# Weights of all experts loaded into the attention's raw weight buffers, and the experts' loops written out

## The reference

```python
x = x + attention(layernorm(x), ctx)      # 64 x 128 tokens of 512; 16 heads of 128, 4 key/value heads,
                                          # q and k RMS-normed, softmax over 128 context rows
x = x + experts(layernorm(x))
def experts(h):                           # T = 8192 tokens, E = 12 experts, top 2, F = 64
    rw, sel = top_k(softmax(h @ gate_w.T), 2); rw = rw / rw.sum(-1)
    for e in range(E):                    # at most cap = ceil(T / E * 1.25) = 854 tokens each
        tok, w = the first cap (token, slot) pairs that chose e
        out[tok] += w * (silu(h[tok] @ w1[e].T * (h[tok] @ w3[e].T)) @ w2[e].T)
```

## Time and profile before

| | |
|---|---|
| three timed runs | 2479.02, 2481.12 (median), 2481.80 us |
| the profiled execution | 2481.03 us, span of its instructions 2479.3 us |
| busy over the span | PE 92%, DVE 76%, ACT 71%, POOL 43% |
| mean granted TensorE clock | 0.963 of 2.4 GHz |
| attention (part one) | from 0 to 2162.2 us |
| experts (part two) | from 2162.3 us to the end |
| DMA | 348 MB, 140 GB/s in the mean |

### The profile page before, as it was taken

How to read it: one execution, slowest core, us unless ns; L and a number is a source line. 1 busy time by engine, 2 the same in 40 slices (tenths; PEclk the granted TensorE clock), 3 DMA queues, 4 the chain that set the end, 5 groups by cost and what they waited for, 6 DMA issues and landing times. The chain is left out here.

```text
span 2479.3 us, 54980 instructions
## 1 busy us (share of the span) xinstructions
PE 2279.2 (92%) x12931; PEld 1143.6 (46%) x12931; DVE 1877.1 (76%) x5158; ACT 1749.1 (71%) x6911; POOL 1055.1 (43%) x1949
## 2 busy tenths in 40 slices
PE   3899999999999999999999999999999999468875
PEld 1344444444444444444444444444444444234442
DVE  6787888888888888888888888888888887436554
ACT  5777777777777777777777777777777777334432
POOL 4333333343343333333443433333333433368875
PEclk9999999999999999999999999999999999878876
DMA  8476666666666666666666666666666666459997
GB/s 254 90 145 138 137 139 135 135 135 136 139 137 136 144 140 138 141 134 136 134 137 137 139 136 140 144 137 138 136 137 135 135 136 126 95 144 188 184 176 92
DMA packets 894359, 348.03 MB, mean 140 GB/s; under 512 B 829004, under 2 KB 829260, under 8 KB 894288
## 3 DMA queue, kind: packets, MB, share of 16 engines
q1 hardware_dynamic: 867520, 297.06, 56.4%
q0 software_dynamic: 22912, 43.16, 9.8%
q10 hardware_dynamic: 3888, 7.38, 0.8%
HBM read 91.37 MB, written 57.71 MB: 60 GB/s over the span
## 5 line engine op out<-in xcount | busy, mean ns | idle before, releaser
L813 PE MATMUL pb<-wo,o 128*128 128x512 f16 x3072 | 708.3, 380 | 21.7 <-DVE o L1065 14.9
L744 PE MATMUL pb<-wq,xT 128*128 128x512 f16 x3072 | 709.0, 381 | 2.1 <-DMA xT<-x 1.2
L943 ACT ACTIVATE work<-pb,small 128x128 f32<-128x128 f32 x1024 | 455.2, 453 | 353.7 <-DVE small L1128 353.7
L1396 POOL TENSOR_TENSOR small<-small 128x4 f32<-128x4 f32 (+1 forms) x584 | 484.1, 833 | 60.9 <-POOL small L1467 18.4
L744 PEld LDWEIGHTS pb<-wq,xT 128*128 128x128 f16 x3072 | 300.8, 98 | 367.3 <-DVE q L1116 13.6
L813 PEld LDWEIGHTS pb<-wo,o 128*128 128x128 f16 x3072 | 286.0, 98 | 357.6 <-DVE o L1065 30.8
L1467 POOL TENSOR_TENSOR small<-small 128x4 f32<-128x4 f32 x256 | 52.1, 203 | 902.0 <-ACT junk_q L924 896.5
L744 PE MATMUL pb<-wkv,cT 128*128 128x512 f16 x1536 | 377.1, 382 | 2.9 <-DVE wkv L1282 2.9
L1116 DVE SCALAR_TENSOR_TENSOR q<-pb,small,q 128x128 f16<-128x128 f32 x1024 | 288.3, 344 | 76.2 <-ACT q L933 76.2
L933 ACT ACTIVATE q<-pb,small 128x128 f16<-128x128 f32 x1024 | 291.1, 366 | 6.3 <-DMA qT<-q 6.3
L1060 DVE TENSOR_TENSOR p<-work,p 128x512 f16<-128x512 f32 x256 | 177.3, 692 | 142.9 <-ACT p L951 137.1
(11 more groups left out here) (146 smaller groups left out, 2887.9 us busy)
## 6 DMA issues: line engine op xcount, KB each, us to landing
work<-x SPq DMA_DIRECT2D x128, 256.0 KB, 2.8
work<-c SPq DMA_DIRECT2D x64, 256.0 KB
out<-work SPq DMA_DIRECT2D x64, 256.0 KB, 2.0
xn_scratch<-work SPq DMA_DIRECT2D x64, 256.0 KB, 2.1
wo_raw<-wo ACTq DMA_DIRECT2D x4, 1024.0 KB, 9.3
qT<-q SPq DMA_TRANSPOSE x256
pT<-p SPq DMA_TRANSPOSE x256
wq_raw<-wq ACTq DMA_DIRECT2D x3, 1024.0 KB, 11.6
```

The lines of the kernel that those rows point to most:

```text
L744: mm = nc.tensor.matmul(bank[:, :], lhs[:, NC * a + c, :], rhs[b_][:, c, :], start=(c == 0 and n == 0), stop=(c == NC - 1 and n == 2))
L813: mm = nc.tensor.matmul(WO_B[:, :], o16[:, HPG * a + h, :], part(O0 + g, b_)[:, h, :], start=(g == 0 and h == 0 and n == 0), stop=(g == NG ...
L943: ex = nc.scalar.activation(probs[:, cols], S_B[:, cols], ACT.Exp, bias=nmax[:, h:h + 1], scale=esc, accum_out=psums[:, h:h + 1])
L1396: return nc.gpsimd.tensor_tensor(out_, in_, neghalf[:, 0:n], ALU.pow)
```

## The change

All twelve experts' weights are loaded once, in part one, into the place of the raw query weights (w13: `w13_all`, 128 x 12 x 4 x 128) and of the raw output weights (w2: `w2_all`, 128 x 12 x 512), which stay allocated through part two. SP issues the three DMAs of an expert at the end of slots 0 and 2 of bodies 2, 61, 62, 63, 64 and 65; ahead of the first it waits for all weights to be split. One semaphore counts them; PE, ACT and DVE wait for all 36 DMAs at the head of part two (PE after the matmul of the totals). The loads, buffers and waits of the weights leave part two, and with them SP's waits for `h_done` and `w2_lo_done`. The loops over pairs of experts of all five engines are written out with constants.

```diff
@@ experts, block.sync
-            def load_w13(j, i):
-                sp.dma_start(w13_s[i][:, :, :], w13[2 * j + i]).then_inc(d_w13[i], 16)
-
-            def load_w2(j, i):
-                for half in (slice(0, F), slice(F, 2 * F)):
-                    sp.dma_start(w2_s[i][half, :], w2T[2 * j + i]).then_inc(d_w2[i], 16)
...
                 wait_apart(sp, (xg_used[1 - i], j + i + 1))
                 load_from(*n)
-                wait_apart(sp, (h_done, 2 * (2 * j + i + 2)))
-                load_w13(*n)
-
-            def ahead_2(j, i):
-
-                wait_apart(sp, (w2_lo_done, 2 * j + i + 1))
-                load_w2(j + 1, i)
...
-            for i in range(2):
-                load_w13(0, i)
-                load_w2(0, i)
             sp.wait_ge(s_n, 1)
...
-            sp.wait_ge(h_done, 2)
-            load_w13(1, 0)
             for i in range(2):
                 ahead_3(0, i)
-                ahead_2(0, i)
                 if i == 1:
                     ahead_1(0, i)
-            with sp.Fori(1, PAIRS - 2) as j:
+            for j in range(1, PAIRS - 2):
                 for i in range(2):
                     ahead_3(j, i)
-                    ahead_2(j, i)
                     ahead_1(j, i)
@@ experts, block.gpsimd
-            with pool.Fori(1, PAIRS - 2) as j:
+            for j in range(1, PAIRS - 2):
@@ experts, block.tensor
-                pe.wait_ge(d_w13[i], 16 * (j + 1))
...
+            pe.wait_ge(d_wexp, 48 * E)
             transposes(0, 0)
             up(0, 0)
             step(0, 0)
             step(0, 1)
-            with pe.Fori(1, PAIRS - 1) as j:
+            for j in range(1, PAIRS - 1):
@@ experts, block.scalar (block.vector likewise)
-                act.wait_ge(d_w2[i], 32 * (j + 1))
...
+            act.wait_ge(d_wexp, 48 * E)
...
-            with act.Fori(1, PAIRS - 1) as j:
+            for j in range(1, PAIRS - 1):
@@ build
+        w13_all = wq_raw[:, :, :, :].rearrange("p g c n -> p (g c n)")[:, 0:E * NC * 2 * F].rearrange(
+            "p (e c n) -> p e c n", e=E, c=NC)
+        w2_all = wo_raw[:, :, :, :].rearrange("p g c n -> p (g c n)")[:, 0:E * HID].rearrange("p (e n) -> p e n", e=E)
...
+                def expert_weights(e):
+
+                    if e == 0:
+                        sp.wait_ge(w_lo, NC * len(SPLIT))
+                    sp.dma_start(w13_all[:, e], w13[e]).then_inc(d_wexp, 16)
+                    for half in range(2):
+                        sp.dma_start(w2_all[half * F:(half + 1) * F, e, :], w2T[e]).then_inc(d_wexp, 16)
+
+                EXPERT_LOADS = {(b, g): ((2 * n + g // 2),) for n, b in enumerate((2, NB - 3, NB - 2, NB - 1, NB, NB + 1))
+                                for g in (0, 2)}
...
                         if g == 3 and live(b - 1):
                             store_xn2(b - 1)
+                        for e in at_slot(EXPERT_LOADS, b, g):
+                            expert_weights(e)
```

More of the change, by code:

```diff
@@ L31, with experts @@
 TINY = 1e-30
-def experts(nc, gt, w13, w2T, out):
+def experts(nc, gt, w13_all, w2_all, out):
     f32, f32r, i32 = mybir.dt.float32, mybir.dt.float32r, mybir.dt.int32
     ACT = mybir.ActivationFunctionType
-    wait, wait_apart, sem, pb, ident, ones_b, macc, xn2_d, table_d = (gt[k] for k in (
-        "wait", "wait_apart", "sem", "pb", "ident", "ones_b", "macc", "xn2_d", "table_d"))
+    wait, wait_apart, sem, pb, ident, ones_b, macc, xn2_d, table_d, d_wexp = (gt[k] for k in (
+        "wait", "wait_apart", "sem", "pb", "ident", "ones_b", "macc", "xn2_d", "table_d", "d_wexp"))
     with ExitStack() as ctx:
@@ L45, in experts @@
         tot, first_n = sb("tot", [128, E]), sb("first_n", [128, E], i32)
-        w13_s = [sb(f"w13_{i}", [128, NC, 2 * F]) for i in range(2)]
-        w2_s = [sb(f"w2_{i}", [2 * F, HID]) for i in range(2)]
         w2_hi, w2_lo, h_parts = sb("w2_hi", [2 * F, HID], f32r), sb("w2_lo", [F, HID], f32r), sb("h_parts", [2 * F, CP], f32r)
@@ L60, in experts @@
         d_join0 = [sem("d_joined_0"), sem("d_joined_1")]
-        d_w13 = [sem(f"d_w13_{i}") for i in range(2)]
-        d_w2 = [sem(f"d_w2_{i}") for i in range(2)]
         d_from = [sem(f"d_from{i}") for i in range(2)]
@@ L163, in _ @@
             for i in range(2):
-                ahead_2(PAIRS - 2, i)
                 ahead_1(PAIRS - 2, i)
@@ L234, in up @@
                     for c in range(NC):
-                        mm = nc.tensor.matmul(H_B[k][:, 0:hi - lo], w13_s[i][:, c, :], xgT[:, c, lo:hi],
+                        mm = nc.tensor.matmul(H_B[k][:, 0:hi - lo], w13_all[:, e, c, :], xgT[:, c, lo:hi],
                                               start=(c == 0), stop=(c == NC - 1))
@@ L312, in split_w2 @@
             def split_w2(j, i):
-                act.wait_ge(d_w2[i], 32 * (j + 1))
                 wait(act, down_done, 2 * j + i)
-                nc.scalar.copy(w2_hi[:, :], w2_s[i][:, :]).then_inc(w2_hi_done, 1)
+                nc.scalar.copy(w2_hi[:, :], w2_all[:, 2 * j + i, :]).then_inc(w2_hi_done, 1)
             def exp_g(j, i):
@@ L371, in silu @@
                         dve.wait_ge(w2_hi_done, e + 1)
-                        nc.vector.tensor_tensor(w2_lo[:, :], w2_s[i][0:F, :], w2_hi[0:F, :].bitcast(f32),
+                        nc.vector.tensor_tensor(w2_lo[:, :], w2_all[0:F, e, :], w2_hi[0:F, :].bitcast(f32),
                                                 ALU.subtract).then_inc(w2_lo_done, 1)
@@ L384, in step @@
                     silu(j + i, 1 - i)
+            dve.wait_ge(d_wexp, 48 * E)
             dve.wait_ge(s_tot, 1)
@@ L393, in _ @@
             step(0, 1)
-            with dve.Fori(1, PAIRS - 1) as j:
+            for j in range(1, PAIRS - 1):
                 step(j, 0)
@@ L455, in build @@
         pb = [psum(f"pb{i}") for i in range(8)]
-        s_table, s_const = sem("s_table_scattered"), sem("s_const")
+        s_table, s_const, d_wexp = sem("s_table_scattered"), sem("s_const"), sem("d_expert_weights")
+        wq_raw = keep.enter_context(nc.sbuf_tensor("wq_raw", [128, NG, NC, 512], f32))
+        wo_raw = keep.enter_context(nc.sbuf_tensor("wo_raw", [128, NG, HPG, HID], f32))
+        w13_all = wq_raw[:, :, :, :].rearrange("p g c n -> p (g c n)")[:, 0:E * NC * 2 * F].rearrange(
+            "p (e c n) -> p e c n", e=E, c=NC)
+        w2_all = wo_raw[:, :, :, :].rearrange("p g c n -> p (g c n)")[:, 0:E * HID].rearrange("p (e n) -> p e n", e=E)
         with ExitStack() as ctx:
@@ L460, in sb @@
                 return ctx.enter_context(nc.sbuf_tensor(name, shape, dt))
-            wq_raw = sb("wq_raw", [128, NG, NC, 512])
             wkv_raw = sb("wkv_raw", [128, 2, NC, 512])
-            wo_raw = sb("wo_raw", [128, NG, HPG, HID])
             wq16 = sb("wq16", [128, 2, NG, NC, 512], f16)
@@ L1590, in build @@
         experts(nc, gt=dict(wait=wait, wait_apart=wait_apart, sem=sem, pb=pb, ident=ident, ones_b=ones_b,
-                            macc=macc, xn2_d=xn2_d, table_d=table_d), w13=w13, w2T=w2T, out=out)
+                            macc=macc, xn2_d=xn2_d, table_d=table_d, d_wexp=d_wexp),
+                w13_all=w13_all, w2_all=w2_all, out=out)
     return nc
```

## The result

| | before | after |
|---|---|---|
| median of the runs (lowest to highest) | 2480.07 us (2477.80 to 2481.80, 4 runs) | 2498.43 us (2496.38 to 2501.24, 4 runs) |
| ratio, 95% interval | | 1.0077 [1.0065, 1.0089] |
| profiled execution, its span | 2481.03, 2479.3 | 2497.99, 2495.9 |
| start of the experts' stage (GpSimd's first instruction) | 2162.3 | 2181.0 |
| from there to the end | 317.0 | 315.0 |

The change makes the kernel 18 us slower, far outside the range of 2473.5 to 2488. All of it is lost ahead of the experts' stage, which starts 18.6 us later; in these two profiles the stage then gives 2.0 back, and the spans differ by 16.6. When both kernels ran on one chip (7 of the experiments) the loss was 16.1 us, ratio 1.0067; there the stage started 17.8 us later and gave nothing back (313.7 us before, 313.9 after).

The account below looks back on a forecast made before the run. It took PE to bound the attention and POOL's issuing the experts' stage. From 2481.03 us: -2.0 (start) - 0.5 (traffic) + 2.9 (kT) + 0.8 (tail) + 0 (loops) = +1.2, so 2482.2; range 2473.5 to 2488.

Parts of the forecast that it names:

- (1): Head of the experts' stage: without weight loads ahead of the first join, the first gather starts 2.0 us earlier.
- (2): Experts' stage: fewer weight transfers under the gathers shorten POOL's instructions by 0.5 us, bounds 0 and 7.
- Rival B: Experts' stage: the DMA engines set the pace, not POOL, so 18 us go: 2464; chance 6%.
- (3): Attention: expert loads in SP's queue delay the keys' turn kT, +2.9 us, bounds 1.5 and 11.1.
- Loads at g = 0: Attention, slot 0: loads ahead of a queries' turn are absorbed by SP's 3.8 us wait for p: cost 0.
- kT is late by 1.5, 0.8 and 0: Attention, loads at g = 2: delay of the keys' turn by SP's issuing in bodies 2, 61 and 62, in us.
- By data: Attention, before kT: an expert's 2.0 us of data must find a gap; 1.4 us late in body 61, fits in 62.
- Rival C: Attention: transposes behind the weights pay the full 3.7 us at three g = 2 places, 11.1 us: 2490; chance 14%.
- (4): Attention's tail: loads of experts 8 to 11 cost 0 to 1 us a place, 0.8 taken, bounds 0 and 3.
- (5): Experts' loops written out: saved branches and extra instruction fetches cost 0, bounds -1 and +3 us.
- A: First expert: the 8.56 us wait vanishes, gather 22 starts 8.4 us earlier: 2473.8; chance 16%.
- D: Head of the experts' stage: the last weights land behind the barrier and hold all engines: 2484; chance under 4%.

Follow-up runs that it names:

- 7 of the experiments: Both kernels unchanged, profiled again on one chip (the second pair of profiles): before 2479.97 us, after 2496.08 us, ratio 1.0067.
- the kernel with one DMA each: Kernel before plus unused loads at all twelve places, one 256 KB DMA (w13) each instead of three: 2484.26 us, ratio 1.0019.
- the unused loads: Kernel before, own loads and loops kept, plus the change's 36 loads in the attention, whose result nobody reads: 2493.44 us, ratio 1.0073.

## Why the prediction was wrong, point by point

**What bounds the kernel** held: PE in the attention, POOL's 0.30 us steps in the experts' stage, in every trace.

**(1) Start of the stage: -2.0 forecast, +0.4 measured.** The sum's logic was right (with the cast early, the clearing releases the first gather). The step that failed is "The three new waits for all weights stand at the head of PE, ScalarE and VectorE ... Cost 0". They hold nobody for long, but in every kernel with the wait at VectorE's head the cast starts later by less than a tenth of a microsecond. Without it, in eight profiles, the cast starts 0.075 to 0.079 us ahead of GpSimd's clearing and takes 0.17; in all six profiled kernels with it, 0.000 to 0.005 us ahead, and the cast takes 3.11, as long as one of the two clearings (3.08). The Trainium skill, SBUF — State Buffer, section SBUF: two separate sides, has an exclusive lock on the port pair that VectorE and GpSimd share, held for the whole instruction by whichever starts first. The trace agrees in the length of the cast, but that this cast is of the kind that takes the pair is argued and not shown. And who starts first in the records isn't always who gets it: in the kernel with one DMA each, without the wait, the cast led by 0.073 us and took 3.18. The forecast's 2.0 us were there to be had at the first gather: with the cast held ahead of the clearing it starts 7.69 us into the stage instead of 9.62. In the total they could not be seen.

**(2) Less traffic under the gathers: -0.5 forecast, nothing that can be shown.** SP's queue falls from 8.7% to 0.8% of the DMA engines' time, their share from 0.94 to 0.89, and POOL's rounds lose 1.6 us from gather 22 on; in the second pair of profiles they gain 2.6. The mean scatter varies from 1569 to 1625 ns among all profiles, with and without loads (1592 before; 1625 with the loops alone written out). Rival B, DMA as the pace, is excluded: its 18 us would have been visible.

**(3) The loads in the attention: +2.9 forecast; measured +13.8 in the three bodies that the sum priced and the block behind the first (+10.9 in the second pair of profiles), and +17.5 (+13.3) up to the last nT.** The last nT itself is 15.9 us late, since kT(2) came 0.7 us earlier and the long loop was 1.0 shorter. The steps that failed:

- "Loads at g = 0 ... the queries are needed a whole slot of 8 us later: cost 0". TensorE needs them a slot later, but ScalarE may not overwrite q16 until the turn has landed, and that reader was never asked. Alone, these loads cost 4.1 us in the four blocks.
- "kT is late by 1.5, 0.8 and 0" by issue, and 2.9 us in all: for the loads at g = 2 alone the pattern held, 1.9, 1.1 and nothing, and what was missed is 1.8 us in the block behind body 2. Body 62, which lost 4.5 us, lost them with the loads at g = 0 in place too.
- "By data ... 2.0 us more must find a gap", the larger of both taken: in the attention the data costs 0 to 0.5 us, the issues 7.4 to 9.0, by the unused loads.
- Body 63 and its experts 6 and 7 are in no term of the sum. They lie in the row from kT(63) to the last nT, with experts 8 and 9: +3.7, in the second pair +2.4.

The two halves of the unused loads, 4.1 and 4.7, add up to the 9.0 of all of them. The changed kernel loses 2 to 5 us more in the same blocks, and why stays open. The prediction's own bound of 11.1 for this term became 6 in the range. Rival C had the sign and missed the mechanism: three full prices for kT, 11.1 us. Its price for one place, 3.7 us, lies near the 3.4 to 4.5 that a body lost, by another road; that is luck.

**(4) The tail: +0.8 forecast (bound 3), 2.9 measured behind the last nT (3.5 in the second pair),** with another 2.0 us of waiting for nT that (3)'s last row holds. The step that failed is "0 to 1 us a place", judged by how thinly used the stretch is. What counted was who waits for a landing there, above all the list scatter that VectorE must see landed. Expert 9, ahead of the last turn of xn2, shows no price of its own.

**(5) Loops written out: 0 forecast, 0 measured** (1.0004 [0.9994, 1.0013]). After, the rows of the DMA queues do have the two instruction queues that before lacks, 3 packets each between 2280 and 2420 us, 0.3% of the engines' time together.

**Rivals.** A: the hole stood, and its size hangs on chip and execution. B fell. D didn't occur: no engine waited for the last weights. The outcome was on C's side of the range; the prediction gave 18% to anything over 2486.1, C's 14% in it, and its range stopped short of C.

## What to carry to other kernels

A DMA put ahead of others in a queue delays the landing of each transfer behind it, and a landing has two readers: who uses the data, and who may then overwrite the source. Look for the second, above all with a single buffer, before a place is costed at nothing. Count a load by its number of issues as well as by its bytes: here one issue of 0.57 us cost 0.3 us an expert, three of 1.7 us together 1.5, and in the attention 16 KB cost as much as 512. Loads belong where the issuing queue waits for something late in any case; there 6.3 MB cost nothing that shows. And check a sum against the list of places: two of the experts' loads had no term here.

## What the runs showed of the hardware

- SP needs 0.57 us to issue a load of 8 KB, as for 256 KB, and 1.15 for two halves of either size.
- A list scatter of 8 bytes a partition landed later with loads issued beside it on another queue: VectorE waited 2.8 to 4.1 us for it with 1 MB in six DMAs, 1.4 to 1.6 with half of that in three, 0.6 with half of that in two issued a little earlier, 0.6 with 32 KB in six, and not at all without.
- A cast of 128x12 elements beside a 3.08 us memset on GpSimd took 0.17 us in the ten profiles in which it led by 0.075 us or more, and 3.11 or 3.18 in the seven in which it led by less.
- Among chips the same kernel had medians of 2472.4 and 2478.2 to 2480.5 us; the four profiles of variants on the faster chip are shorter between gather 1 and gather 22 (29.5 to 31.1 us against 34.6 to 39.7).
